# Cross-attention with short heads: slot 0's closing steps interleaved with slot 1's column scores

## The reference

```python
x = x + tanh(g_xattn[0]) * L0_xattn(_layernorm(x), ctx, ...)   # 16 heads of 8, Wo, bo
x = x + tanh(g_ffn[0])   * L0_ffn(_layernorm(x), ...)          # layernorm, gamma, beta, act_quant, w1, gelu, act_quant, w2
...
x = x + tanh(g_xattn[3]) * L3_xattn(_layernorm(x), ctx, ...)   # 16 heads of 8, Wo

attn = softmax(einsum('bqhd,bkhd->bhqk', Q, K) * 8 ** -0.5)
y = einsum('bhqk,bkhd->bqhd', attn, V).reshape(B, xN, DIM) @ Wo

def act_quant(x):                                              # one scale for each token
    scale = 127.0 / clip(max(abs(x), axis=-1), EPS)
    return clip(round(x * scale), -128, 127), scale
```

## Time and profile before

| | |
|---|---|
| median of 3 runs | 1880.04 us |
| all three | 1881.96, 1880.04, 1859.07 us |
| the profiled execution: its time, its span | 1865.42 us, 1863.7 us |
| busy: PE, DVE, ACT, POOL | 1597.1 (86%), 886.3 (48%), 728.7 (39%), 147.9 (8%) us |
| mean granted clock of TensorE, full being 1 | 0.874 |

### The profile page before, as it was taken

One profiled execution on the slowest core, in us unless ns is written; L12 is line 12 of the kernel. 1 busy time (PEld: TensorE's weight loads), 2 busy tenths in 40 slices (PEclk: granted clock), 3 DMA queues, 4 the chain that ended last, 5 costly groups with the idle time before them and its releaser, 6 DMA issues.

```text
span 1863.7 us, 22238 instructions
## 1 busy us (share of the span) xinstructions
PE 1597.1 (86%) x8922; PEld 739.3 (40%) x8924; DVE 886.3 (48%) x1710; ACT 728.7 (39%) x1279; POOL 147.9 (8%) x207
## 2 busy tenths in 40 slices
PE   5948999879899989987659999898899989888387
PEld 2322323332344435733324322342444437543284
DVE  4283686253456343234555784342664442437312
ACT  2334555323545224242344554433454134243033
POOL 0000111100012000000000112000011000002321
PEclk8568899989999688987778999899998789889688
DMA  4000000000000100000000000000000100020241
GB/s 184 1 0 1 1 1 1 1 0 1 0 1 1 46 1 0 1 1 2 1 1 1 1 1 1 1 1 0 1 1 1 46 0 1 1 74 5 67 138 60
DMA packets 18106, 30.15 MB, mean 16 GB/s; under 512 B 4640, under 2 KB 12640, under 8 KB 17104
## 3 DMA queue, kind: packets, MB, share of 16 engines
q1 hardware_dynamic: 16752, 26.10, 4.3%
q0 software_dynamic: 1248, 2.59, 0.4%
HBM read 23.49 MB, written 5.19 MB: 15 GB/s over the span
## 4 chain that ended last, share of the span: by engine, by line
PE 77%; DVE 12%; ACT 7%; issue 2%; DMA 1%; POOL 1%; SPq 0%; POOLq 0%; DVEq 0%; ACTq 0%
PE ps L817 7%; PE ps L910 4%; PE ps L682 4%; PE ps L852 3%; PE ps L627 3%; PE ps L1356 3%; PE ps L1368 3%; PE ps L1040 3%; PE ps L721 3%; PE ps L961 3%; PE ps L941 2%; PE ps L865 2%; PE ps L1048 2%; PE ps L659 2%; PE ps L842 2%
## 5 line engine op out<-in xcount | busy, mean ns | idle before, releaser
L2039 DVE TENSOR_REDUCE peak<-ps 128x1 f32<-128x512 f32 x256 | 164.1, 686 | 93.6 <-PE ps L817 92.0
L1656 ACT ACTIVATE big<-ps 128x512 f32<-128x512 f32 x256 | 140.9, 595 | 125.1 <-PE ps L844 123.6
L842 PE MATMUL ps<-qT,pp 32*128 32x512 f32 x512 | 162.2, 659 | 0.0
L817 PE MATMUL ps<-pp,qT 32*128 32x512 f32 x512 | 150.7, 673 | 1.4 <-ACT pp L1762 1.4
L1679 ACT ACTIVATE big<-ps 128x512 f32<-128x512 f32 (+3 forms) x256 | 101.2, 437 | 116.8 <-PE ps L941 115.8
L2084 DVE TENSOR_REDUCE crest<-ps 128x2 f32<-128x512 f32 (+3 forms) x128 | 104.9, 825 | 61.6 <-PE ps L916 61.5
L941 PE MATMUL ps<-qT,pp 32*128 32x384 f32 (+3 forms) x512 | 130.7, 521 | 2.3 <-ACT big L1679 1.4
L1610 ACT ACTIVATE big<-ps 77x1024 f32<-77x1024 f32 x96 | 93.4, 1017 | 89.1 <-PE ps L682 88.6
L1966 DVE TENSOR_REDUCE small<-ps 128x8 f32<-128x616 f32 x96 | 74.3, 798 | 91.3 <-PE ps L655 53.5
L910 PE MATMUL ps<-pp,qT 32*128 32x384 f32 (+3 forms) x512 | 105.4, 480 | 5.3 <-DVE crest L2084 2.7
L1590 ACT ACTIVATE sq<-ps 128x512 f32<-128x512 f32 x48 | 28.7, 597 | 180.4 <-PE ps L627 180.4
(11 more groups left out here) (480 smaller groups left out, 2777.7 us busy)
## 6 DMA issues: line engine op xcount, KB each, us to landing
big<-in_w SPq DMA_DIRECT2D x23, 256.0 KB, 3.1
pt<-in_l2w SPq DMA_DIRECT2D x2, 2048.0 KB, 7.7
w_l<-in_l SPq DMA_DIRECT2D x1, 3086.0 KB, 17.2
pp<-in_w SPq DMA_DIRECT2D x1, 2048.0 KB, 9.8
big<-by_expert SPq DMA_DIRECT2D x23, 66.0 KB, 1.9
by_expert<-cst SPq DMA_DIRECT2D x1, 1472.0 KB, 16.0
cst<-in_const SPq DMA_DIRECT2D x1, 1299.0 KB, 5.7
w_l<-in_l SPq DMA_DIRECT2D x1, 1218.0 KB, 7.8
```

What stands on the lines that cost most here:

```text
L817: pe.matmul(rbank(x), qT[at, u, k, 128 * i:128 * i + 128], keyT(u, k)[at, :], start=True, stop=True, tile_position=(32 * c, 0)).then_inc(* ...
L842: pe.matmul(tbank(y), keyT(u, k)[at, 128 * j:128 * j + 128], qT[at, u, k, :], start=True, stop=False, tile_position=(32 * c, 0))
L1656: A(prob(m)[:, TURN_OF[g], :], tbank(tplace(m, g)), ACT.Exp).then_inc(*SCALAR.did("a1", "exp", m, g))
L2039: v.tensor_reduce(peak[:, p // 4 % 2, i, c:c + 1], rbank(ring(p, c)), AX.X, ALU.max)\
```

## The change

Three things are done in the two calls with dh = 8. (1) Slot 1's column steps take the places 26, 27, 29, 30, 32, 33, 35, 36: two pairs of banks (6, 7 and 2, 3), while the pair 4, 5 stays free for slot 0. (2) Slot 0's `heads`, `inverses` and its product with Wo (now `outward`, L647 in the new program) stand between slot 1's column scores, and in layer 0 its transposes between slot 1's `heads`. VectorE's order follows: slot 0's division and residual ahead of slot 1's first joining, and slot 0's statistics and scaling between slot 1's steps. (3) The first quantisation, the transposes back and the first product of the quantised layer are done slot by slot. `ybank`, `xtbank` and `q1bank` say where the moved results go.

```diff
             if (kind == "R") == (u == 0):
-                return a if u == 0 else 26 + a
+                return a if u == 0 else 26 + a if dh == 32 else 26 + 3 * (a // 2) + a % 2
...
             if z > 25:
-                return "T", 1, z - 26
+                return "T", 1, z - 26 if dh == 32 else 2 * ((z - 26) // 3) + (z - 26) % 3
...
+        def ybank(u):
+            return PSB[4] if u == 0 else PSB[1]
+        def xtbank(u):
+            return PSB[5] if u == 0 else PSB[7]
+        def q1bank(u):
+            return PSB[4] if u == 0 else PSB[7]
...
+                def outward(u):
+                    pe.wait_ge(*VECTOR[tag, "o", u])
+                    pe.matmul(ybank(u), wo, xn[:, u, :], start=True, stop=True).then_inc(*TENSOR.did(tag + " y", u))
...
                 def free_late(x):
-                    pe.wait_ge(*SCALAR[tag, "exp", 1, x - 29])
+                    pe.wait_ge(*(SCALAR[tag, "exp", 1, 6] if x == 35 else SCALAR[tag, "shift", 1]))
...
                 turned(1)
+                if dh == 8:
+                    colscores4(1, 0)
+                    heads(0, 0)
+                    colscores4(1, 1)
+                    values(1, 0)
+                    heads(0, 1)
+                    colscores4(1, 2)
+                    values(1, 1)
+                    inverses(0)
+                    colscores4(1, 3)
+                    values(1, 2)
+                    outward(0)
+                    values(1, 3)
+                    heads(1, 0)
+                    if tokens_first:
+                        tokens_first(0)
+                    heads(1, 1)
+                    inverses(1)
+                    outward(1)
+                    if tokens_first:
+                        tokens_first(1)
+                    return
...
-                if dh == 8:
-                    heads(0, 0)
-                    heads(0, 1)
                 sums(1, 3)
                 values(1, 3)
-                if dh == 8:
-                    heads(1, 0)
-                    inverses(0)
-                    heads(1, 1)
-                    inverses(1)
-                    return
...
-                token_rstd("l0f a")
+                token_rstd("l0f a", 0)
                 act.wait_ge(*VECTOR["l0f rounded", 50, 0])
                 A(tq(0), xn[:, 0, :], ACT.Identity, bias=K["unmagic"]).then_inc(*SCALAR.did("l0f q1", 0))
+                token_rstd("l0f a", 1)
...
                 if dh == 8:
-                    for u in U:
-                        joined(u, 0)
-                        if u:
-                            divided(0)
-                        else:
-                            joined(0, 1)
-                            head_inverse(0)
+                    joined(0, 0)
+                    joined(0, 1)
+                    head_inverse(0)
+                    divided(0)
+                    residual_of(0)
+                    joined(1, 0)
+                    if tokens:
+                        stats, applied, scaled = tokens
+                        stats(0)
                     head_inverse(1)
                     joined(1, 1)
+                    if tokens:
+                        applied(0)
                     divided(1)
+                    residual_of(1)
+                    if tokens:
+                        scaled(0)
                     return
...
+                cross("l0x", 8, residual_of, W["l0"]["bv"], (stats, applied, scaled))
+                stats(1)
+                turned_back(0)
+                applied(1)
+                hidden_of(0)
+                scaled(1)
+                turned_back(1)
+                hidden_of(1)
...
+                cross("l3x", 8, residual_of)
```

More of the change, by code:

```diff
@@ L1712, in experts, with token_rstd @@
                     A(sq[:, u, :], aux(u), ACT.Identity).then_inc(*SCALAR.did(tag + " rep", e, u))
[L1714 to L1722, removed]
+            def token_rstd(tag, u):
+                act.wait_ge(*VECTOR[tag, "st", u])
+                A(sm(u, 44, 4), sm(u, 32, 8).rearrange("p (a b) -> p a b", b=2)[:, :, 1], ACT.Ln, bias=K["eps twice"],
+                  scale=1.0 + EPS)\
+                    .then_inc(*SCALAR.did())
+                act.wait_ge(*SCALAR.last())
+                A(sm(u, 44, 4), sm(u, 44, 4), ACT.Exp, scale=-0.5).then_inc(*SCALAR.did(tag, "r", u))
             act.wait_ge(loaded["const"], 16)
@@ L2211, in experts, with token_stats, token_norm @@
                         v.tensor_tensor(a, a, t, ALU.add).then_inc(*VECTOR.did(tag + " out", e, u))
[L2213 to L2219, removed]
-                    last.then_inc(*VECTOR.did(tag, "st", u))
-                for u in U:
-                    v.wait_ge(*SCALAR[tag, "r", u])
-                    for i in range(4):
-                        last = v.tensor_scalar(xn[:, u, 128 * i:128 * i + 128], src(u)[:, 128 * i:128 * i + 128],
-                                               sm(u, 32 + 2 * i, 1), sm(u, 44 + i, 1), ALU.subtract, ALU.mult)
-                    last.then_inc(*VECTOR.did(tag, "n", u))
+            def token_stats(tag, src, u):
+                for i in range(4):
+                    ins = v.bn_stats(sm(u, 6 * i, 6), src(u)[:, 128 * i:128 * i + 128])
+                chain(ins)
+                for i in range(4):
+                    last = v.bn_aggr(sm(u, 32 + 2 * i, 2), sm(u, 6 * i, 6))
+                last.then_inc(*VECTOR.did(tag, "st", u))
+            def token_norm(tag, src, u):
+                v.wait_ge(*SCALAR[tag, "r", u])
+                for i in range(4):
+                    last = v.tensor_scalar(xn[:, u, 128 * i:128 * i + 128], src(u)[:, 128 * i:128 * i + 128],
+                                           sm(u, 32 + 2 * i, 1), sm(u, 44 + i, 1), ALU.subtract, ALU.mult)
+                last.then_inc(*VECTOR.did(tag, "n", u))
             def quantise(name, u, src, dst, mw, at):
@@ L2283, in _, with residual_of, stats, applied @@
                         .then_inc(*VECTOR.did("l0x", "q", u))
-                cross("l0x", 8, W["l0"]["bv"])
                 v.wait_ge(gated, 1)
-                for u in U:
+                def residual_of(u):
                     v.wait_ge(*TENSOR["l0x y", u])
-                    residual("l0x res", u, lin(u), 0, W["l0"]["bo"])
-                for u in U:
+                    residual("l0x res", u, ybank(u), 0, W["l0"]["bo"])
+                def stats(u):
                     v.wait_ge(*TENSOR["l0f xt", u])
-                token_norm("l0f a", lambda u: aux(u))
-                for u in U:
-                    v.wait_ge(*VECTOR.last())
+                    token_stats("l0f a", xtbank, u)
+                def applied(u):
+                    token_norm("l0f a", xtbank, u)
+                def scaled(u):
+                    v.wait_ge(*VECTOR["l0f a", "n", u])
                     x3 = xn[:, u, :].rearrange("p (i f) -> p i f", i=4)
```

28 lines of the change are left out of this document (12 added, 16 removed).

## The result

| | kernel before | changed kernel |
|---|---|---|
| median of 20 runs each | 1859.21 us | 1864.82 us |
| lowest to highest | 1843.13 to 1881.96 | 1850.1 to 1880.04 |
| ratio, with its 95% interval | | 1.0065 (1.0038 to 1.0093) |
| profiled execution: time, span, mean clock | 1865.42, 1863.7, 0.874 | 1867.8, 1866.1, 0.869 |

Timed once more in 12 runs beside 17 of the kernel before, the medians were 1866.59 and 1863.11. Over all runs of this study (32 and 118) the means differ by 5.6 us (1.2 to 10.0, worked out from their spread). So the change costs about 0.3%: small, but probably not nothing.

A forecast was written before the change was run, and what follows sets the result against it. TensorE's order, and VectorE's where the chain runs over it, was taken to bound the kernel, with the clock mattering as much. 1865.4 - 4 + 13.5 = 1875 and 1880 - 4 + 9 = 1885 gave 1880 us, range 1858 to 1902.

The forecast's parts named there:

- The level: Whole kernel: 1875 us from the profiled execution, 1885 from the median shown, 1880 taken between the two.
- -4 and +13.5: Whole kernel: reordering saves 4 us over four calls; clock falling to half costs 4.5 in each of three fast calls.
- The ring: Slot 1's column scores: two bank pairs for three make groups 3.3 us in place of 2.31, last values +2.1.
- The tail of layer 3: Layer-3 call, last values to the copy: 11 to 12 us, not 13.6; whole call -0.3.
- -1.7 - 0.7: Layer-3 tail: slot 0's inverses leave it (1.7 us), and slot 1's product no longer waits behind slot 0's (0.7).
- Layer 0: Layer-0 call and the quantised layer's first half: -1.7 us per call in all.
- VectorE's part: Quantised layer behind slot 1's residual: statistics, scaling and a wait leave, new waits of 1.3 come, -2.0 us.
- The clock in slot 1's groups: Clock falls to half in slot 1's first or second column-score group, +4.5 us for each of three fast calls.
- the order alone, at the clocks of before up to the last values: All four calls: reordering without new clock changes gives 2 x -0.3 + 2 x -1.7 = -4 us.
- Clock stays down: Three fast calls: half clock until slot 1's product, +9 us each; 1888 or 1903 us, chance 0.2.
- clock holds: Fast calls: full clock through slot 1's groups, tail 3 us less each; 1852 or 1867 us, chance 0.12.
- The sign: Whole kernel: sum goes from 1865.4 to 1875, slower, but within what a measurement tells; "same" had chance 0.96.

The follow-up runs named there:

- ring_only: Kernel before with only the two-pair bank ring for slot 1's column scores and its waits, every order as before; 1872.54 us, ratio 1.0126.
- l0_only: Kernel before with the change in the two layer-0 calls and the quantised layer alone, layer 3 as before; 1853.63 us, ratio 0.9968.
- a_rows: Changed kernel with extra matmul products, never read, only in slot 0's row scores and around the transposes of the maxima; 1845.45 us, ratio 0.9959 to kernel before.
- l3_only: Kernel before with the change in the two layer-3 calls alone, layer 0 as before; 1869.71 us, ratio 1.0079.
- a_six: Changed kernel with six copies that nobody reads at the end of VectorE's part of each turn; 1851.18 us, ratio 0.9938 to kernel before.
- a_two: Changed kernel with two copies that nobody reads at the end of VectorE's part of each turn; 1865.35 us, ratio 1.0068 to kernel before.
- b_two: Kernel before with two copies that nobody reads at the end of VectorE's part of each turn; 1876.39 us, ratio 1.0026.
- b_warm: Kernel before with 23 extra matmul products per call, never read, in TensorE's holes in row scores, transposes and tail; 1840.83 us, ratio 0.9907.
- b_rows: Kernel before with extra matmul products, never read, only in slot 0's row scores and around the transposes of the maxima; 1849.07 us, ratio 0.9979.

## Why the prediction was wrong

- **The level.** 1880 was the middle between 1875, summed from the profiled execution, and 1885, from the median of three. Three runs whose times lie up to 23 us apart don't give the level; 20 have it at 1859. From there the same sum (-4 and +13.5) gives 1869; measured 1865 to 1867. That this is near is luck: the 13.5 stood for falls in three calls, and the runs have 15 in one call, at another place.
- **The ring**: forecast +2.1 to the last values and groups of 3.3; measured 2.08 and 3.33; ring_only 2.5 and 3.13. Right. The moved steps fitted, and slot 0's product had its quotient in time.
- **The tail of layer 3**: forecast 11 to 12, measured 9.3, so -2.15 per call and not -0.3. The term "-1.7 - 0.7" was too small: it left slot 1's sums and inverses at half clock. In the changed kernel the clock is full until 834.8, behind them (sums 1.06 us for the 1.88 of before, inverses 1.16 for 2.06), so part of the -2.15 is the clock's.
- **Layer 0**: forecast -1.7, taken at the clock of before. Measured where both begin alike, though the clock of the tails differs: 91.15 to 89.10, -2.05 (l0_only's second turn, at full behind its first 12 us), and 106.84 to 106.32, -0.5 (first turn before, second turn after, both at half). VectorE's part was -2.0, measured -2.2.
- **The clock in slot 1's groups**: the price, +4.5, was right (4.45 in a_rows; 3.8 in three layer-3 calls of l3_only, a_six and a_two). How often was wrong: in the changed kernel's two profiles no layer-3 call fell there; only layer-3 calls whose first fall came late did (8.6 us: three of three of the new form; 5.3: none of seven). The one call that did as forecast is the layer-0 call of the first turn, in both profiles: at full from 63.5, it fell at 70.3, in slot 1's second group, for 10.1 us, and was back ahead of slot 0's inverses (L759 at 80.99), which the prediction had bring it back. That call was at half before, and so not one of the three priced. "I expect it to fall to half in the first or second group" was tied to the narrow sums, and the layer-3 calls have the sums without the fall.

```profile
63.50:70.20 6.70, 5.50 (x48) 2.33 (x44) 2.43 (x5) 3.50 (x6) 0.00 (x0) 1.00 0.00 0
70.30:80.40 10.10, 10.10 (x48) 3.51 (x48) 1.74 (x3) 3.98 (x5) 0.00 (x0) 0.50 0.01 2
```

- **The step that failed**: "the order alone, at the clocks of before up to the last values", with 3 x 4.5 on top. It took the clock of the row scores as given, call by call, though nothing in the rows says that a call keeps its clock when it starts at another time; a change there was put at nothing without a reason, although the 15 us between the two layer-0 calls had been read. The change shortens the layer-3 call by 2.15 us and the gap by 0.5; the next layer-0 call begins 65.7 and not 68.35 us behind, and lands where the clock does not come back: +15 us, more than the order gives in the four calls together (2 x 2.15 and 2 x 0.5 to 2.05). The profiles of a_six (start given back: half for 6.8 us, and a median 13.6 us lower) and of b_two (start moved, order untouched: half for 41 us) show it from both sides, with one execution of each.
- **The rivals.** "Clock stays down" (0.2) named half clock as the danger, but in the groups and from their narrow sums; "clock holds" is what layer 3 did. The sign was that of the sum, +9.5 on the profiled execution, for another reason than the one given: luck, not insight.

Left open: why a fall at 4.3 to 4.8 us is followed by no return, and one at 5.1 to 5.4 by a quick one. The runs show the outcomes, and that in the five profiles with products in the row scores no call fell there; the rule behind them they don't show. The first turn's layer-0 call varies in all profiles, by a start that nothing here sets.

## What to carry to other kernels

Where the granted clock falls inside a call, the call's time can depend on when it begins, and shortening what stands before it can cost more than it gives: compare calls at equal granted clock, first row to last, before judging an order by the total. Look for stretches in which TensorE waits for another engine ahead of a dense phase, and feed it there with products into a free bank, one place at a time (b_warm's products in the tail made its layer-3 call 1.1 us longer than b_rows'); feeding was worth some four times as much here as the order (21 us against 5), and it narrows the spread. Take the level from many runs, and the mean clock of each run beside its time.

## What the runs showed of the hardware

- TensorE stayed at 1.2 GHz for 51 us in which it was busy 47.8 us, mostly with products over 32 or 77 rows, between two stretches at full (changed kernel, 858.8 to 909.9); the same instructions, started 2.7 us later against the call before, ran at full after 6.8 us (a_six).
- With the start 0.4 us later (68.35 to 68.77) the same call took 12.7 us longer, to the end of the feed-forward (before and b_two, one execution each).
- 15 extra 128x128 by 512 bf16 products in the row scores (b_rows) cost no more than the clock that they kept gave: the last column score comes at 35.4 us and not at 35.74.
- A wait of 0.84 us and one of 1.10 in 4.5 us of wide column scores stood ahead of a fall (ring_only, 885.49 to 890.04), and in a twin with the same two waits no fall came (layer 3, full up to 824.0).
